# An audio tower kernel: block 13's down products in parts, block 15's W_down halves later, second pass's first high weights ahead of block 14's units, and weight loads in another order

## The reference

```python
def _L0_tok_ref(x, W, b):                  # P = 128, stride 64
    patches = x[:, idx, :].reshape(B, starts.shape[0], P * F)
    return jnp.einsum('bnp,dp->bnd', patches, W) + b
...
def _L0_attn_ref(hidden_states, Wq, Wk, Wv, Wo):
    q, k, v = (proj(Wq), proj(Wk), proj(Wv))
    q, k = _rope(q, k, s, d, hidden_states.dtype)
    scores = jnp.einsum('bhqd,bhkd->bhqk', q, k) / math.sqrt(d)
    scores = jnp.maximum(scores + causal, neg)
    tmp_attn = jax.nn.softmax(scores.astype(jnp.float32), axis=-1).astype(scores.dtype)
    tmp_sum = jnp.sum(tmp_attn, axis=-2)
    _, topk_idx = jax.lax.top_k(tmp_sum, heavy_budget)
...
    scores = jnp.where(mask, scores, neg)   # heavy keys or within the band
    probs = jax.nn.softmax(scores.astype(jnp.float32), axis=-1).astype(q.dtype)
    attn = jnp.einsum('bhqk,bhkd->bhqd', probs, v)
    return attn @ Wo.T
...
def _L0_ffn_ref(h_shard, w_gate_up, w_down):
    gate, up = jnp.split(jnp.einsum('bsh,oh->bso', h_shard, w_gate_up), 2, axis=-1)
    return jnp.einsum('bsi,hi->bsh', jax.nn.silu(gate) * up, w_down)
...
    h = _L0_tok_ref(x, L0_tok_W, L0_tok_b)
    h = h + _L0_attn_ref(_layernorm(h, axis=-1), L0_attn_Wq, L0_attn_Wk, L0_attn_Wv, L0_attn_Wo)
    h = h + _L0_ffn_ref(_layernorm(h, axis=-1), L0_ffn_w_gate_up, L0_ffn_w_down)
```

## Time and profile before

| | us |
|---|---|
| median of 3 runs | 268.63 |
| lowest, highest | 267.50, 268.77 |
| the profiled execution | 268.19 |
| its span in the trace | 266.4 |

### The profile page before, as it was taken

One profiled execution on the slowest core, in us unless ns is written; L12 is line 12 of the kernel. 1 busy time (PEld: TensorE's weight loads), 2 busy tenths in 40 slices (PEclk: granted clock), 3 DMA queues, 4 the chain that ended last, 5 costly groups with the idle time before them and its releaser, 6 DMA issues.

```text
span 266.4 us, 5045 instructions
## 1 busy us (share of the span) xinstructions
PE 257.1 (96%) x1909; PEld 213.5 (80%) x1909; DVE 169.9 (64%) x333; ACT 108.2 (41%) x181; POOL 48.9 (18%) x53
## 2 busy tenths in 40 slices
PE   7999999799999999989999999999999999999993
PEld 5466498575887887867888879999999999999992
DVE  1696998997899987899976775633333333343323
ACT  2311212863285454749531053533443333344320
POOL 0116032004001121100100101422222222222210
PEclk9999999999999999999999999999999999999999
DMA  6996003005359999983890050694333344400004
GB/s 220 416 418 220 1 4 122 2 2 100 59 161 232 290 252 288 271 270 135 219 285 12 0 198 5 168 336 127 119 118 118 118 121 126 128 19 0 0 0 118
DMA packets 13154, 38.61 MB, mean 145 GB/s; under 512 B 1864, under 2 KB 1936, under 8 KB 12496
## 3 DMA queue, kind: packets, MB, share of 16 engines
q1 hardware_dynamic: 11120, 32.17, 35.2%
q0 software_dynamic: 1728, 5.81, 11.5%
q10 hardware_dynamic: 288, 0.39, 0.4%
HBM read 31.24 MB, written 1.31 MB: 122 GB/s over the span
## 4 chain that ended last, share of the span: by engine, by line
PE 78%; DMA 8%; DVE 6%; ACT 3%; issue 3%; SPq 1%; POOL 0%; DVEq 0%; POOLq 0%
PE ps L225 49%; PE ps L1345 5%; PE ps L1223 5%; PE ps L1118 4%; DMA wgu<-stage 3%; PE ps L1326 3%; DMA stage<-w_ffn 3%; PE ps L1238 3%; PE ps L1185 3%; PE ps L1144 2%; DMA dims<-w_dims 2%; PE ps L1127 1%; PE ps L1069 1%; PE ps L1155 1%; DVE xT L724 1%
## 5 line engine op out<-in xcount | busy, mean ns | idle before, releaser
L225 PE MATMUL ps<-xT,wgu 128*128 128x384 f32 x384 | 70.5, 339 | 0.2 <-DVE gu L931 0.2
L225 PEld LDWEIGHTS ps<-xT,wgu 128*128 128x128 f32 x384 | 68.1, 188 | 1.8 <-issue 0.6
L931 DVE TENSOR_TENSOR gu<-silu,ps 128x256 f32<-128x256 f32 (+1 forms) x32 | 15.5, 485 | 47.5 <-PE ps L225 44.4
L363 POOL TENSOR_TENSOR wd<-stage,wd 128x512 fp32r<-128x512 f32 x16 | 26.2, 1636 | 77.1 <-ACT wd L431 77.1
L225 PE MATMUL ps<-wd,hT 128*128 128x512 f32 x156 | 38.8, 393 | 0.0
L591 ACT ACTIVATE silu<-ps 128x256 f32<-128x256 f32 (+1 forms) x32 | 14.0, 437 | 52.7 <-PE ps L225 52.2
L225 PEld LDWEIGHTS ps<-wd,hT 128*128 128x128 f32 x156 | 29.0, 188 | 5.4
L225 PE MATMUL ps<-xs,wgu 128*128 128x256 f32 x240 | 31.9, 289 | 0.9 <-DMA wgu<-stage 0.9
L225 PEld LDWEIGHTS ps<-xs,wgu 128*128 128x128 f32 x240 | 28.8, 188 | 4.6 <-issue 4.1
L431 ACT ACTIVATE wgu<-stage 128x1024 fp32r<-128x1024 f32 x20 | 21.1, 1056 | 24.4 <-PE ps L225 23.1
L1345 PE MATMUL ps<-stage,gu 128*128 128x512 f32 x56 | 26.3, 593 | 0.0
(11 more groups left out here) (126 smaller groups left out, 318.3 us busy)
## 6 DMA issues: line engine op xcount, KB each, us to landing
stage<-w_ffn SPq DMA_DIRECT2D x32, 512.0 KB, 4.5
stage<-w_ffn SPq DMA_DIRECT2D x32, 256.0 KB, 4.0
wgu<-stage POOLq DMA_DIRECT2D x6, 512.0 KB, 8.3
wd<-stage POOLq DMA_DIRECT2D x3, 512.0 KB, 7.0
stage<-w_k SPq DMA_DIRECT2D x1, 1024.0 KB, 6.6
stage<-w_q SPq DMA_DIRECT2D x1, 1024.0 KB, 10.1
stage<-w_v SPq DMA_DIRECT2D x1, 1024.0 KB, 12.1
wo<-w_o SPq DMA_DIRECT2D x1, 1024.0 KB, 15.2
```

The lines of the kernel that those rows point to most:

```text
L225: ins = pe.matmul(dst, lhs[a], rhs[b], start=first and n == 0, stop=last and n == 2)
L363: pool.tensor_tensor(dst, src, f32(hi), ALU.subtract).then_inc(done, 1)
L931: dve.tensor_tensor(gu[:, ring, cols], silu[:, ring, cols], ps[:, up, at:at + P * TILES[p]], ALU.mult)\
```

## The change

Six things are changed.

1. The number of first-pass blocks whose down product is in parts becomes three: SD = 13 takes the place of S0 = 14 in down_whole, low_units, low_weights_down and the semaphore counts (ND for NS).
2. W_down halves: block 13's and 14's are made where 14's and 15's were; block 15's are made after the token casts (ScalarE) and after block 15's product (DVE).
3. The high part of the second pass's first gate/up weights, hi_gu(0, 0, 0), goes ahead of block 14's units on ScalarE; hi_gu(1, 1, 1) goes ahead of hi_down(0, 0, 0).
4. SP's loads: gate/up 6 and 7 (next_gate_up(2), (3)) ahead of 4 and 5, and the down loads further back.
5. ScalarE: hi_attn(0) ahead of minus_weights(2).
6. DVE: of softmax part 3 only the mask stands ahead of softmax_out(2); the rest of softmax_in(3) and statistics(3) follow the products of queries 7 to 4. ScalarE's exponentials are not moved.

```diff
+SD = 13
+ND = NB - SD
...
             def next_down(i):
-                if i < S0:
+                if i < SD:
                     sp.wait_ge(down_mm[A], i + 1)
                 else:
-                    sp.wait_ge(wd_lo, i - S0 + 1)
+                    sp.wait_ge(wd_lo, i - SD + 1)
                 down_load((i + SLOTS) % NB)
...
+            next_gate_up(2)
+            next_gate_up(3)
             next_gate_up(0)
-            for i in range(1, NB):
+            next_gate_up(1)
+            next_down(0)
+            for i in range(4, S2 + 1):
+                next_gate_up(i)
+                next_down(i - 3)
+            next_gate_up(S2 + 1)
+            next_down(S2 - 2)
+            next_down(S2 - 1)
+            next_down(S2)
+            for i in range(S2 + 2, NB):
                 next_gate_up(i)
                 next_down(i - 1)
             next_down(NB - 1)
...
                 act.wait_ge(dma_down[i % SLOTS], down_count(A, i, i % SLOTS))
+                if i == SD + 2:
+                    act.wait_ge(down_mm[A], SD + 1)
                 hi_down(i, i % 2, i % SLOTS)
...
+            hi_attn(0)
             minus_weights(2)
-            hi_attn(0)
             hi_attn(1)
...
             hi_weights(14)
-            hi_weights_down(14)
+            hi_weights_down(13)
             first_pass(13)
             hi_weights(15)
-            hi_weights_down(15)
+            hi_weights_down(14)
...
-            first_pass(14)
+            silu_gate(A, 14, 0)
             hi_gu(0, 0, 0)
+            hi_units(14)
             hi_xT(LN2[2])
             hi_xT(LN2[4])
             hi_xT(LN2[3])
+            hi_weights_down(15)
             first_pass(15)
             act.wait_ge(down_mm[A], NB - 1)
             act.wait_ge(dma_down[0], down_count(Z, 0, 0))
+            hi_gu(1, 1, 1)
+            act.wait_ge(wd_lo, ND)
             hi_down(0, 0, 0)
-            hi_gu(1, 1, 1)
...
             softmax_in(2)
-            softmax_in(3)
+            mask(SOFTMAX[3][2])
             softmax_out(2)
             values(0, 7, 6, 5, 4)
+            softmax_in(3, unmasked=False)
+            statistics(3)
             softmax_out(3)
             values(0, 3, 2, 1, 0)
-            statistics(3)
             statistics(4)
...
             first_pass(13)
             low_weights(14)
+            low_weights_down(13)
+            low_units(13)
+            low_weights(15)
             low_weights_down(14)
-            low_weights(15)
-            low_weights_down(15)
...
             first_pass(15)
+            low_weights_down(15)
             low_units(15)
```

More of the change, by code:

```diff
@@ L350, in _ @@
                       .then_inc(dma_stage[u], 16)
-                    sp.wait_ge(wd_lo, SLOTS * n + (NS + u + 1))
+                    sp.wait_ge(wd_lo, SLOTS * n + (ND + u + 1))
                     sp.dma_start(stage[:, u, 2 * KT * P:FW],
@@ L395, in lo_down @@
             def lo_down(i, ring, slot):
-                pool.wait_ge(wd_hi, i + (NS + 1))
+                pool.wait_ge(wd_hi, i + (ND + 1))
                 low(wd[:, ring, 1], stage[:, slot, 2 * KT * P:FW], wd[:, ring, 0], wd_lo)
@@ L594, in first_pass, with hi_units @@
                 silu_gate(A, i, i % 2)
-                if i >= S0:
-                    act.wait_ge(gu_prod[A], i + 1)
-                    split_hi(hT[:, i % 2, 0, 0:2 * P], gu[:, i % 2, 0:2 * P], hT_hi)
+                if i >= SD:
+                    hi_units(i)
+            def hi_units(i):
+                act.wait_ge(gu_prod[A], i + 1)
+                split_hi(hT[:, i % 2, 0, 0:2 * P], gu[:, i % 2, 0:2 * P], hT_hi)
             def second_pass(i, u, first=False, next_gu=True, next_down=True):
@@ L613, in second_pass @@
                         act.wait_ge(down_mm[Z], i)
-                        act.wait_ge(wd_lo, i + NS)
+                        act.wait_ge(wd_lo, i + ND)
                     act.wait_ge(dma_down[(u + 1) % SLOTS], down_count(Z, i + 1, (u + 1) % SLOTS))
@@ L800, in rows, with softmax_in @@
                 return x[:, slice(*part)].rearrange("p i h j -> p (i h) j")
-            def softmax_in(n):
+            def softmax_in(n, unmasked=True):
                 g, masked, part = SOFTMAX[n]
                 if masked:
-                    mask(part)
+                    if unmasked:
+                        mask(part)
                 elif not g:
@@ L954, in low_weights_down @@
                 slot, ring = i % SLOTS, i % 2
-                dve.wait_ge(wd_hi, i - S0 + 1)
+                dve.wait_ge(wd_hi, i - SD + 1)
                 dve.tensor_tensor(wd[:, ring, 1], stage[:, slot, 2 * KT * P:FW], f32(wd[:, ring, 0]), ALU.subtract).then_inc(wd_lo, 1)
             def low_units(i):
-                dve.wait_ge(hT_hi, i - S0 + 1)
+                dve.wait_ge(hT_hi, i - SD + 1)
                 dve.tensor_tensor(hT[:, i % 2, 1, 0:2 * P], gu[:, i % 2, 0:2 * P], f32(hT[:, i % 2, 0, 0:2 * P]), ALU.subtract)\
@@ L970, in second_pass @@
                 up_product(Z, i, ring)
-                dve.wait_ge(hT_hi, i + (NS + 1))
+                dve.wait_ge(hT_hi, i + (ND + 1))
                 dve.tensor_tensor(hT[:, ring, 1], gu[:, ring], f32(hT[:, ring, 0]), ALU.subtract).then_inc(hT_lo, 1)
@@ L1333, in down_whole @@
                 last = i == NB - 1
-                if i >= S0:
-                    pe.wait_ge(hT_lo, i - S0 + 1)
-                    pe.wait_ge(wd_lo, i - S0 + 1)
+                if i >= SD:
+                    pe.wait_ge(hT_lo, i - SD + 1)
+                    pe.wait_ge(wd_lo, i - SD + 1)
                 else:
@@ L1370, in down @@
             def down(i, ring, first=False, last=False):
-                pe.wait_ge(hT_lo, i + (NS + 1))
-                pe.wait_ge(wd_lo, i + (NS + 1))
+                pe.wait_ge(hT_lo, i + (ND + 1))
+                pe.wait_ge(wd_lo, i + (ND + 1))
                 for u in range(TILES[Z]):
```

## The result

The changed kernel is slower. Its median is 273.15 us (271.87 to 273.35, 6 runs) against 268.7 us (267.5 to 271.71, 6 runs) of the kernel before: ratio 1.016, 95% interval 1.012 to 1.020. The forecast was 272.3 us with a range of 270.3 to 273.3. The profiled execution of the changed kernel is its quickest, 271.87 us with a span of 270.1 us, 3.7 us more than that of before. What decides the time is the sixth of the six changes, the order of DVE's softmax.

A forecast was written before the change was run, and what follows sets the result against it. TensorE, busy for 96% of the span, was taken as the bound. Terms +3.87 - 0.88 - 0.34 - 0.21 = +2.44 us on 268.63, plus 1.2 for the clock, gave 272.3 us; range 270.3 to 273.3.

The forecast's parts named there:

- Part 1: DVE's softmax order, group 0: value_sums(0) starts 4.21 us later, behind ScalarE's k_all copies; transposes return 0.34, net +3.87 us.
- The clock: TensorE's clock falls during its 5.64 us wait before value_sums(0); price between 0 and 1.74 us, 1.2 taken.
- Part 2: SP's load queue: earlier gate/up loads remove TensorE's wait for block 10's weight sum, -0.88 us, bounds 0 and 0.88.
- Parts 3 and 4: Block 13's down product as six fp32r records, -0.34 us; hi_gu(0) moved into ScalarE's wait at block 14, -0.21 us.
- The 2 us of the text: ScalarE: leaving minus_weights(2) with its two casts ahead of hi_attn(0) would cost some 2 us more.
- Faster: Before value_sums(0): k_all copies not behind exponential(3) on the path, TensorE starts 0.80 us earlier; 266.4 us, chance 0.04.
- Clock holds, 271.1: Same wait before value_sums(0), but TensorE's clock stays full: 271.1 us, chance 0.32.
- Loads do not do what they say: SP's reordered loads: the 0.88 us stays or shows up at another block; 272.0 to 273.2 us, chance 0.08.
- Half absorbed: Half of the delay before value_sums(0) is absorbed by something held tight, the layer norm chain: 269.5 us, chance 0.04.

The follow-up runs named there:

- moving the one line: Changed kernel with exponential(3) on ScalarE moved behind the six copies of k_all and q_all: 267.77 us, ratio 0.995 to the kernel before.
- two other kernels with the same wait of 5.6 us: Kernel before with DVE's new softmax order alone, 274.97 us; changed kernel with hi_attn(0) put back behind block 2's weight casts, 273.42 us.
- the filler run: Changed kernel with 24 extra fp32 matmuls on TensorE in the wait ahead of value_sums(0): 271.55 us, ratio 1.009 to the kernel before.

## Why the prediction was right, and where it was off

- **The wait (Part 1).** Right to 0.1 us behind the start-up (0.17 us earlier in this trace): exponential(3) at 55.65 was forecast and was at 55.53, the start of value_sums(0) at 57.37 and was at 57.16, with a start-up 0.17 us earlier. Against before it starts 6.68 - 2.51 = 4.17 us later behind the projection; 4.21 was forecast. It was found in one place of the trace, the order of ScalarE behind a moved producer on DVE; taking the order back and moving the one line both confirm it.
- **The clock.** The forecast was that it falls; it did, in all six executions (mean clock 0.985 to 0.987). The price was left between 0 and 1.74, and 1.2 was taken. It was 1.67 in the profiled execution, and 2.3 and 2.9 in the traces of two other kernels with the same wait of 5.6 us. This is the term that was sized too small. The reasoning behind it was wrong as well: the upper end took the low stretch at the start of the kernel (3.47 us) as the longest possible, and in three traces TensorE worked at the low level for longer, up to 6.0 us. The choice of 1.2 inside the bounds rested on no row. A fall later in the wait leaves more of the 6.8 us of low clock to the work behind it. The other five executions took 272.61 to 273.35 us with no trace kept of them; that a later fall makes their difference to 271.87, and the 0.85 us that the median lies above the forecast, is likely and not shown.
- **The loads (Part 2).** Right in mechanism, undersized. The idle bracket of 0.88 us is counted from the modelled end of the matmul before. From down product to down product the block took 119.80 - 114.22 = 5.58 us instead of 4.46 (rows of the kernel before, TensorE's timeline):

```profile
114.22 1.88 PE L1345 MATMUL ps<-stage,gu 128*128 128x512 f32 x4
116.99 2.98 PE L225 MATMUL ps<-xs,wgu 128*128 128x256 f32 x24 [0.88 <-DMA wgu<-stage]
119.80 1.88 PE L1345 MATMUL ps<-stage,gu 128*128 128x512 f32 x4
```

  So the wait cost 1.12 us. And 0.28 us came back as the wait of block 11, which was not forecast: DVE's product of block 11 ended 0.70 us ahead of the down product before (128.02 and 128.72), less than the 1.12 that TensorE gained.
- **Block 13 and ScalarE at block 14 (Parts 3 and 4).** -0.34 and -0.21 us were forecast. From block 14's gate/up to the second pass's start it was 159.63 - 149.29 = 10.34 us before and is 163.40 - 153.75 = 9.65: -0.69 us. Block 13's part is 0.32 us of it, 0.34 forecast. The extra again is the wait's bracket: 0.21 us idle, but 1.75 - 1.38 = 0.37 us in the step.
- **hi_attn(0).** The 2 us of the text, had the swap not been made, were wrong in size and in kind: 1.2 us in the step (0.8 at the end) with the clock full, and no wait with the clock low.
- **The sum.** Forecast for the profiled execution: 4.21 - 0.34 + 1.2 - 0.88 - 0.34 - 0.21 = +3.64. By the trace: 4.17 - 0.34 + 1.67 - 1.12 + 0.28 - 0.69 = +3.97, and measured +3.87 behind the projection. That the profiled execution came out at 271.87 us where 268.19 + 3.64 = 271.83 was forecast is partly luck: the clock cost 0.47 us more, the part products and ScalarE's order at block 14 gave 0.14 more, and the start-up happened to be 0.17 us shorter.
- **The rivals.** Faster (the copies do not stand behind the exponential): out by the row at 55.53. Clock holds, 271.1: out by the 5 in the clock's row; the filler run, where it holds, has 271.55. Loads do not do what they say: out by the waits of the queue. Half absorbed: out, the steps from 61.70 us to the first down product are the same 19.97 us in the changed kernel (81.67) and with the filler (61.10 to 81.07), and 20.0 before.

## What to carry to other kernels

When a step is moved on one engine, look at what the engines that consume it have queued behind it in their order: here a gain of 0.8 us on DVE cost 4.2 on TensorE, because a small exponential stood ahead of copies that needed nothing of it.
- A wait on a semaphore in front of a short stream costs more than its bracket: 0.88 us in the bracket, 1.12 us in the step; 0.21 and 0.37.
